# Perceiver block on one core: softplus and the choice of experts spread out in the fourth batch of a tile

## The chip, the core and the metric

One core of one Trainium2 chip runs the whole program. The metric is the device time in microseconds; lower is better. The engines are called as in the profile: PE (TensorE), DVE (VectorE), ACT (ScalarE), POOL (GpSimd), SP (SyncE, which only starts transfers here).

## The reference

The inputs are `x` (128 sequences of 32 tokens of width 256), a context of 257 tokens for each sequence, a mask, and float32 weights. Three layers follow one another, each with a layer norm before it and a residual after it:

```python
x = x + xattn(layernorm(x), ctx, mask)   # 16 heads of 16; softmax over 257 context tokens
x = x + ssd(layernorm(x))                # in this use only batch 0's states are read: out = Y[0] / norm
x = x + moe(layernorm(x))                # 8 experts, top 2, hidden 704, silu gate
```

Two small pieces of it matter here. In the second layer `dt = softplus(dt + dt_bias)`, `A = A_param * dt`, and `cumA = cumsum(A)` over the 32 tokens. In the third the router's 8 logits of each token give the two largest and their numbers, and a one-hot row of 8 for each.

## The kernel before

**Stages.** The first stage (about 1000 us) does the attention, the second layer and the routing of all 4096 tokens. It goes over 32 tiles of 128 tokens; a tile has four batches `b` (one sequence each, all 16 heads). The second stage (about 470 us) runs 71 slots of 128 tokens through the experts. The change is in the first stage alone.

**Order of the work.** Each engine has its instructions in one order written out by hand, and the engines meet at semaphores. Tiles 0 to 3 and 29 to 34 are unrolled on DVE and PE, tiles 4 to 28 are a hardware loop. The work of one tile is spread over several: while tile `i` is in attention, tile `i-1` is in the output projection, second layer norm, `softplus` and cumulative sum, and tile `i-2` in the third norm, the logits and the choice of experts. In batch `b` of tile `i` DVE does the score maxima of the next batch (`maxima`, one operation for each of four groups, L879), copies the keys of the batch after next from PSUM (`take_keys`, two operations, L868), and takes the attention output of this batch (`take_output`: `om`, L892, then `ou`, L894).

**The fourth batch** (`b == 3`). DVE also computes `softplus` of tile `i-1` on vectors of 128x16 in the tile `dtv`. With `u = exp(-|x|)` from ACT it makes `y = u/(u+2)` (`softplus_ratio`, L964 to L966), squares it and starts a polynomial (`softplus_series`, L972 and L973), does six more steps of it (L976, called k1 to k6 below), and closes with L980, L981 and L984. Every one of these reads what the one before wrote and waits for its semaphore. L984 increments `a_done`. In the same batch `take_logits` (L1023) copies the logits of tile `i-2` out of the PSUM bank `M`, and `select` does six operations on 128x8 or smaller (L1028 to L1039).

**PE in the fourth batch**: the scores of the next batch, the keys of the one after (`k`), the router, the weighted values, four transposes of the probabilities, `turn_z1(i+2)` (two transposes into `M`, L493, after `lg_done` of the logits), `project_v` (12 products), four more transposes, and last `sum_a(i-1)`, a product with 128x16 that waits first for `z1T_done` and then for `a_done`. Behind it stands the first batch of the next tile, which begins with its scores.

**ACT in the fourth batch**: exponentials of the four groups, `take_probs`, then `take_rp` (a 32x32 copy that waits for `ou_done`), `take_z1T` (which gives `z1T_done`), `take_values`, `take_probs`, and `decays` after `sum_a`.

**POOL**: in the third batch it does the first norm of tile `i+2` (L1239), in tiles 4 to 27 also `piece_low` (L1289, a 128x512 subtraction that prepares 1/24 of the experts' down weights), then, for the next batches, `split_low` (L1249, 128x516) and `lay_queries` (L1257 and L1261).

Of the kernel before, what the change touches and what calls it, by code (L numbers as in the profile page):

```python
# [8 lines left out]
ALU = mybir.AluOpType  # L9
# [7 lines left out]
NH = D // P  # L17
# [22 lines left out]
ATANH = [2 * k + 1 for k in range(7, 0, -1)]  # L40
# [20 lines left out]
def held(eng, met, *waits):  # L61


    for _, value in waits:
        if not isinstance(value, int):
            eng.compute_val(value)
    eng.wait_ge(*met)
    for sem, value in waits:
        at_least(eng, sem, value)
# [40 lines left out]
def runs(i):  # L110

    return not isinstance(i, int) or 0 <= i < NT


def attend(nc, xd, ctxd, ctxl, maskd, pard, wxbcd, cond, padd, wgd, wud, wdd, d_high, d_low, zbuf, table, outd, con, cst, wg, wu, wd,
# [7 lines left out]
    with own:  # L123
# [71 lines left out]
        dtv = sb("dtv", [P, 11, H])  # L195
# [12 lines left out]
        def carve(n):  # L208
# [47 lines left out]
        dt_ready, dt_done, nabs_done, u_done, soft, a_done = (sem("dt_ready"), sem("dt_done"), sem("nabs_done"),  # L256
                                                              sem("u_done"), sem("soft"), sem("a_done"))
# [12 lines left out]
        init, soft_sum, soft_max = sem("init"), sem("soft_sum"), sem("soft_max")  # L270
        NSOFT = len(ATANH) + 5
# [587 lines left out]
        def _(dve):  # L859
            V = nc.vector  # L860

            def take_keys(i, b):

                n = 4 * i + b
                at_least(dve, s_ready, 4 * n - 4)
                dve.wait_ge(k_ready, n + 1)
                for a in range(NH):
                    V.tensor_scalar(kT[:, b % 2, a, 0:LAST], K2[:, a, :], prm("bk")[:, a:a + 1], None, ALU.add  # L868
                                    ).then_inc(k_done, 1)

            def maxima(i, b, *groups):
                n = 4 * i + b
                for g in groups:
                    if g == 0:

                        held(dve, (init, 2), (msk_in[b], 64 * (i + 1)), (exp_done, 4 * n), (s_ready, 4 * n + 1))
                    else:
                        held(dve, (init, 2), (s_ready, 4 * n + g + 1))
                    V.tensor_tensor_reduce(sm[:, g, :], SC[g][:, 0:S], msk[:, b, :], -1.0, 3.0e38, ALU.add, ALU.min,  # L879
                                           nmx[:, g:g + 1]).then_inc(max_done, 1)  # L880
# [5 lines left out]
                V.reciprocal(rr[:, 0, :], rsum[:, :]).then_inc(rec_done, 1)  # L886

            def take_output(i, b):
                n = 4 * i + b
                dve.wait_ge(o_ready, n + 1)  # L890
                at_least(dve, ou_done, n)
                V.tensor_scalar(om[:, :, :], OT[:, :, 0, :], own2[:, 0:1], None, ALU.mult).then_inc(om_done, 1)  # L892
                dve.wait_ge(om_done, n + 1)
                V.scalar_tensor_tensor(ou[:, :, b * Q:(b + 1) * Q], OT[:, :, 1, :], own2[:, 1:2], om[:, :, :],  # L894
                                       ALU.mult, ALU.add).then_inc(ou_done, 1)
# [58 lines left out]
            su, sr, sy, sw, ss = dtv[:, 2, :], dtv[:, 3, :], dtv[:, 4, :], dtv[:, 8, :], dtv[:, 9, :]  # L954

            def link(ins, j, k):

                ins.then_inc(soft, 1)
                dve.wait_ge(soft, NSOFT * j + k)
# [8 lines left out]
            def softplus_series(j, first, last):  # L968

                if first == 0:  # L970
                    dve.wait_ge(soft, NSOFT * j + 3)
                    link(V.tensor_tensor(sw, sy, sy, ALU.mult), j, 4)  # L972
                    V.tensor_scalar(ss, sw, 1.0 / ATANH[0], None, ALU.mult).then_inc(soft, 1)  # L973
                for k in range(max(first, 1), last):
                    dve.wait_ge(soft, NSOFT * j + 4 + k)
                    V.scalar_tensor_tensor(ss, ss, 1.0 / ATANH[k], sw, ALU.add, ALU.mult).then_inc(soft, 1)  # L976

            def softplus_end(j):
                dve.wait_ge(soft, NSOFT * j + NSOFT - 1)
                link(V.scalar_tensor_tensor(ss, ss, 1.0, sy, ALU.add, ALU.mult), j, NSOFT)  # L980
                V.scalar_tensor_tensor(sw, ss, 2.0, dtv[:, 10, :], ALU.mult, ALU.add).then_inc(soft_sum, 1)  # L981
                dve.wait_ge(soft_sum, j + 1)
                at_least(dve, cum_ready, j)
                V.tensor_tensor(dtv[:, 5, :], sw, prm("apar"), ALU.mult).then_inc(a_done, 1)  # L984
# [36 lines left out]
            def take_logits(j):  # L1021
                dve.wait_ge(lg_ready, j + 1)
                V.tensor_copy(lg[:, 0, :], M[:, 0:E]).then_inc(lg_done, 1)  # L1023

            def select(j):

                held(dve, (init, 2), (lg_done, j + 1))
                V.max(lg[:, 1, :], lg[:, 0, :]).then_inc(top_done, 1)  # L1028
                held(dve, (init, 2), (top_done, j + 1))
                V.max_index(mi[:, :], lg[:, 1, :], lg[:, 0, :]).then_inc(index_done, 1)  # L1030
                V.tensor_tensor(sv[:, 0, 0:1], lg[:, 1, 1:2], lg[:, 1, 0:1], ALU.subtract).then_inc(diff_done, 1)
                dve.wait_ge(index_done, j + 1)
                V.tensor_copy(sv[:, 2, :], mi[:, 0:TOPK]).then_inc(expert_done, 1)
                dve.wait_ge(expert_done, j + 1)
                V.tensor_tensor(oh[:, :, :], cst("iota8").unsqueeze(1).broadcast_to([P, TOPK, E]),
                                sv[:, 2, :].unsqueeze(2).broadcast_to([P, TOPK, E]), ALU.is_equal).then_inc(oh_done, 1)
                dve.wait_ge(oh_done, j + 1)
                at_least(dve, chosen_done, j + 1)
                V.tensor_tensor(lg[:, 2, :], oh[:, 0, :], oh[:, 1, :], ALU.add).then_inc(mm_done, 1)  # L1039
# [103 lines left out]
            def tile(i):  # L1143
                for b in range(TB):
                    nxt, two = following(i, b), following(i, b, 2)
                    if b == 3 and runs(i - 1):
                        softplus_ratio(i - 1)
                        softplus_series(i - 1, 0, 1)
                    if runs(nxt[0]):
                        maxima(*nxt, 0, 1)  # L1150
                    if runs(nxt[0]):
                        maxima(*nxt, 2, 3)
                    if b == 0 and runs(i - 1):
                        weigh(i - 1)
                    if b == 2 and runs(i + 1):
                        take_queries(i + 1)
                    if b == 3 and runs(i - 2):
                        take_logits(i - 2)
                    if runs(two[0]):
                        take_keys(*two)  # L1160
                    if runs(i):
                        take_output(i, b)
                    if b == 3 and runs(i - 1):
                        softplus_series(i - 1, 1, len(ATANH))
                    if b == 0 and runs(i - 1):
                        attention_out(i - 1)
                    if b == 1 and runs(i - 1):
                        normalise2(i - 1)
                    if b == 2 and runs(i - 2):
                        normalise3(i - 2)  # L1170
                    if b == 3 and runs(i - 1):
                        softplus_end(i - 1)
                    if runs(nxt[0]):
                        reciprocals(*nxt)
                    if b == 3 and runs(i - 2):
                        select(i - 2)
                    if b == 0 and runs(i - 2):
                        norms(i - 2)
                    if b == 0 and runs(i - 3):
                        take_ranks(i - 3)  # L1180
                    if b == 0 and isinstance(i, int) and i == 2:
                        ssd()
                    if b == 1 and runs(i - 2):
                        residual2(i - 2)
                    if b == 2 and runs(i - 1):
                        soft_in(i - 1)
                    if b == 0 and runs(i - 2):
                        scale_y(i - 2)
                    if b == 1 and runs(i - 3):
                        place(i - 3)  # L1190
                    if b == 1 and runs(i + 2):
                        statistics1(i + 2)
                    if b == 0 and runs(i - 1):
                        residual1(i - 1)
                        statistics2(i - 1)
# [16 lines left out]
                V.tensor_scalar(kl[:, a, :], M2K[:, a, :], prm("bk")[:, a:a + 1], None, ALU.add).then_inc(vl_done, 1)  # L1212
            take_queries(0)
            statistics1(1)
            take_keys(0, 0)
            maxima(0, 0, 0, 1, 2, 3)
            take_keys(0, 1)
            dve.wait_ge(own_done, 1)
            reciprocals(0, 0)
            steps(dve, tile)  # L1220
# [488 lines left out]
```

## Time and profile before

| | |
|---|---|
| median of 3 runs | 1527.64 us (1525.33 to 1528.3) |
| the profiled execution's own time | 1529.16 us |
| its span | 1527.2 us |
| busy: PE, DVE, ACT, POOL | 93%, 74%, 66%, 55% |
| granted PE clock, mean | 0.969 |

The span is the stretch from the first to the last instruction of the profiled execution; some 2 us of that execution lie outside it. The busy shares are means over both stages.

### The profile page before, as it was taken

What the parts mean: (1) busy time and instruction counts of PE and PEld (TensorE: products, weight loads), DVE (VectorE), ACT (ScalarE), POOL (GpSimd) and SP (SyncE); (2) the same over time, 40 slices, a digit from 0 to 9 for tenths busy, and PEclk for the clock granted to TensorE, in tenths of its full rate; (3) what the DMA queues carried; (4) which work ended last, traced back from release to release, by engine and by line L of the source; (5) the groups of instructions that cost most, each with busy time, mean ns of one, the idle gap of its engine ahead of it and who ended that gap; (6) DMA issues with size and microseconds to landing.
All of it is one profiled execution on the core that took longest, in us unless ns stands there. A gap on an engine that the chain in (4) does not pass through costs nothing.

```text
span 1527.2 us, 53971 instructions
## 1 busy us (share of the span) xinstructions
PE 1422.5 (93%) x15668; PEld 1294.9 (85%) x15669; DVE 1125.5 (74%) x3967; ACT 1000.9 (66%) x2482; POOL 838.1 (55%) x1401
## 2 busy tenths in 40 slices
PE   6969999999999999999999999649999999999997
PEld 5858888888888888888888888449999999999997
DVE  3647777777777777777777777557877787787775
ACT  4726766767766766766766676237777777677674
POOL 4514655655655655565565554226665666566554
PEclk9969999999999999999999999569999999999999
DMA  5302544554333343343343331425555555556554
GB/s 187 81 12 81 167 140 130 165 159 128 110 103 90 98 114 90 88 119 88 97 117 86 87 81 41 180 78 160 143 162 140 155 145 160 138 144 161 137 141 111
DMA packets 102009, 183.81 MB, mean 120 GB/s; under 512 B 19392, under 2 KB 61376, under 8 KB 101792
## 3 DMA queue, kind: packets, MB, share of 16 engines
q1 hardware_dynamic: 86272, 164.35, 35.2%
q0 software_dynamic: 15680, 18.76, 7.0%
q8 instruction: 29, 0.48, 0.1%
q14 instruction: 28, 0.23, 0.0%
HBM read 152.63 MB, written 31.13 MB: 120 GB/s over the span
## 4 chain that ended last, share of the span: by engine, by line
PE 72%; DVE 8%; issue 6%; ACT 2%; DMA 2%; POOL 1%; POOLq 1%; DVEq 0%; ACTq 0%; SPq 0%
PE m L412 12%; PE k L412 10%; PE y_p L1420 9%; PE v_p L412 9%; PE up_p L1420 8%; PE gate_p L1420 8%; PE sc L412 7%; PE pt L471 5%; PE ht_p L1459 3%; DVE dtv L976 2%; DMA par<-zbuf,gi 2%; ACT wd L735 1%; PE m L493 1%; PE z_p L1426 1%; DVE kT L868 1%
## 5 line engine op out<-in xcount | busy, mean ns | idle before, releaser
L735 ACT ACTIVATE wd<-wd,nmx 128x257 f32<-128x257 f32 x512 | 254.7, 499 | 100.6 <-DVE nmx L879 97.2
L879 DVE CUSTOM_DVE_ANT_0 wd<-sc,wd 128x257 f32<-128x257 f32 x512 | 187.3, 422 | 56.1 <-PE sc L412 45.8
L1622 POOL DMA_INDIRECT out<-par,oi x71 | 113.5, 1599 | 146.7 <-ACT par L1528 146.1
L1249 POOL TENSOR_TENSOR ctx_lo<-wd,ctx_hi 128x516 fp32r<-128x516 f32 x128 | 165.3, 1291 | 48.9 <-ACT ctx_hi L711 44.1
L711 ACT ACTIVATE wd<-pt 128x512 f32<-128x512 f32 x256 | 151.5, 592 | 57.9 <-PE pt L471 57.7
L471 PE MATMUL pt<-con,wd 128*128 128x128 f32 x1024 | 161.0, 280 | 3.0 <-ACT wd L735 0.7
L412 PE MATMUL k<-ctx_hi,wkh 128*128 128x256 f32 x512 | 158.2, 309 | 1.4 <-POOL ctx_lo L1249 1.4
L412 PE MATMUL v_p<-wvh,ctx_hi 128*128 128x256 f32 x512 | 158.0, 309 | 0.5 <-ACT y L711 0.5
L1499 ACT ACTIVATE uw_hi<-wu 128x1408 fp32r x71 | 98.3, 1385 | 85.1 <-PE up_p L1420 84.8
L1610 POOL COPY oi<-par 128x4 int32 x71 | 148.2, 2088 | 0.0
L1557 DVE TENSOR_TENSOR uw_lo<-wu,uw_hi 128x1408 fp32r<-128x1408 f32 x71 | 115.4, 1626 | 41.2 <-ACT uw_hi L1499 41.2
L412 PE MATMUL k<-ctx_lo,wkh 128*128 128x256 f32 x512 | 144.7, 283 | 0.0
L412 PE MATMUL v_p<-wvh,ctx_lo 128*128 128x256 f32 x512 | 144.6, 282 | 0.0
L412 PE MATMUL k<-ctx_hi,wkl 128*128 128x256 f32 x512 | 144.4, 282 | 0.0
L1557 DVE TENSOR_TENSOR gw_lo<-wg,gw_hi 128x1408 fp32r<-128x1408 f32 x71 | 115.4, 1625 | 39.3 <-ACT gw_hi L1499 39.3
L412 PE MATMUL v_p<-wvl,ctx_hi 128*128 128x256 f32 x512 | 143.9, 281 | 0.0
L412 PEld LDWEIGHTS k<-ctx_hi,wkh 128*128 128x128 f32 x512 | 96.4, 188 | 50.5 <-issue 48.7
L1610 POOL COPY gi<-par 128x4 int32 x71 | 122.3, 1722 | 9.5 <-issue 5.7
L1267 POOL TENSOR_TENSOR rr<-wd,rr 128x4 f32<-128x4 f32 x128 | 25.6, 200 | 178.9 <-DVE rr L886 178.9
L1420 PE MATMUL y_p<-wd,hT_hi 128*128 x426 | 121.0, 284 | 1.9 <-DVE hT_lo L1557 1.9
L471 PEld LDWEIGHTS pt<-con,wd 128*128 128x128 f32 x1024 | 113.0, 140 | 10.1 <-ACT wd L735 5.9
L1420 PE MATMUL y_p<-wd,hT_lo 128*128 x426 | 120.4, 283 | 0.0
(197 smaller groups left out, 4662.2 us busy)
## 6 DMA issues: line engine op xcount, KB each, us to landing
dl<-d_low SPq DMA_DIRECT2D x71, 768.0 KB, 4.4
wd<-in_ctx SPq DMA_DIRECT2D x128, 258.0 KB, 2.8
wd<-in_mask SPq DMA_DIRECT2D x512, 32.1 KB, 1.8
wd<-in_wd SPq DMA_DIRECT2D x24, 256.0 KB, 3.0
d_high<-wd SPq DMA_DIRECT2D x24, 256.0 KB, 2.0
d_low<-wd SPq DMA_DIRECT2D x24, 256.0 KB, 2.3
wd<-d_high SPq DMA_DIRECT2D x8, 768.0 KB, 9.1
wg<-in_wg SPq DMA_DIRECT2D x8, 704.0 KB
```

The costliest lines, as they stand in the source:

```text
L412: return nc.tensor.matmul(out, lhsT, rhs, start=start, stop=stop)
L471: last = nc.tensor.transpose(PT[:, o:o + P], pr[:, g, t * P:(t + 1) * P], ident)
L711: return nc.scalar.activation(out, in_, ACT.Copy, **kw)
L735: nc.scalar.activation(pr[:, g, :], sm[:, g, :], ACT.Exp, bias=nmx[:, g:g + 1], scale=-1.0, accum_out=rsum[:, g:g + 1]).then_inc(exp_done, 1)
L879: V.tensor_tensor_reduce(sm[:, g, :], SC[g][:, 0:S], msk[:, b, :], -1.0, 3.0e38, ALU.add, ALU.min, nmx[:, g:g + 1]).then_inc(max_done, 1)
L1249: G.tensor_tensor(ctx_lo[:, b % 2], ctx[:, b], ctx_hi[:, b % 2].bitcast(F32), ALU.subtract).then_inc(lo_done, 1)
L1420: return nc.tensor.matmul(out, lhsT, rhs, start=start, stop=stop)
L1459: last = nc.tensor.transpose(HB[k][:, (c % 4) * P:(c % 4 + 1) * P], hb[:, c * P:(c + 1) * P], ident)
L1499: nc.scalar.activation(dst, src, ACT.Copy).then_inc(done, 1)
L1557: V.tensor_tensor(dst, src, hi.bitcast(F32), ALU.subtract).then_inc(done, 1)
L1610: G.tensor_copy(dst.unsqueeze(1), tab[:, bass.ds(col, 1), :]).then_inc(done, 1)
L1622: G.indirect_dma_start(outd[:, :], bass.IndirectOffsetOnAxis(oi[:, s, 1:2].bitcast(U32), 0), yb[:, s, :], None, compute_op=ALU.add).then_i ...
```

## The change

The steps of `softplus` and of `select` are no longer done as blocks. `take_keys` and `take_output` are cut into their single operations, `softplus_end` and `select` into functions of one or two operations, and in the fourth batch they alternate. All operations, their operands and their semaphores stay; only their order on DVE changes, in the fourth batch alone. The other engines' programs are the same.

```diff
-            def take_keys(i, b):
+            def take_keys(i, b, *chunks):
...
-                for a in range(NH):
+                for a in chunks:
...
             def take_output(i, b):
+                first_head(i, b)
+                second_head(i, b)
...
+            def softplus_log(j):
+                dve.wait_ge(soft, NSOFT * j + NSOFT - 1)
+                V.scalar_tensor_tensor(ss, ss, 1.0, sy, ALU.add, ALU.mult).then_inc(soft, 1)
+
+            def softplus_sum(j):
+                dve.wait_ge(soft, NSOFT * j + NSOFT)
+                V.scalar_tensor_tensor(sw, ss, 2.0, dtv[:, 10, :], ALU.mult, ALU.add).then_inc(soft_sum, 1)
...
             def softplus_end(j):
...
                 dve.wait_ge(soft_sum, j + 1)
                 at_least(dve, cum_ready, j)
                 V.tensor_tensor(dtv[:, 5, :], sw, prm("apar"), ALU.mult).then_inc(a_done, 1)
```

The order on DVE in the fourth batch of a tile in the loop, one operation or group of operations after another (`k1` is `softplus_series(i-1, 1, 2)`, and so on; `top` is `V.max`; `index` is `V.max_index` and the subtraction behind it; `number` is the cast of the two numbers; `log`, `sum`, `end` are L980, L981, L984):

```
before: ratio square | max0 max1 max2 max3 | logits | keys0 keys1 | om ou | k1 k2 k3 k4 k5 k6 | log sum end |
        reciprocals | top index number one_hot both
after:  ratio square | max0 max1 k1 max2 k2 max3 k3 | logits k4 | keys0 k5 top | keys1 k6 index | om log ou |
        sum number end one_hot | reciprocals | both
```

## Rows read from the trace of the kernel before

**Rows 1.** Waits of PE over the whole span: total us, times, longest.

```profile
PE m L412 <- DVE dtv L984: 16.4, 28, 2.5
PE sc L412 <- issue: 14.8, 27, 0.8
```

**Rows 2.** Windows: tiles 5 to 27 of the loop, then one unrolled tile; each engine's busy us.

```profile
188.70:856.80 668.10, 641.07 (x8632) 559.91 (x8631) 520.08 (x2502) 462.02 (x1423) 389.96 (x803) 1.00 0.39 114
...
886.00:914.00 28.00, 27.87 (x384) 24.41 (x390) 21.75 (x108) 19.22 (x60) 15.53 (x35) 1.00 0.29 73
```

**Rows 3.** Timeline of PE in tile 19, fourth batch: start us, us, line, tiles, count, idle before.

```profile
620.98 0.38 PE L493 MATMUL m<-con,wd 128*128 128x128 f32 x2
...
622.62 0.60 PE L471 MATMUL pt<-con,wd 128*128 128x128 f32 x4
623.68 0.37 PE L412 MATMUL m<-dtv,con 128*128 128x16 f32 x2 [0.47 <-DVE dtv L984]
624.59 0.69 PE L412 MATMUL sc<-kT,qbd 32*64 32x257 f32 x16 [0.54 <-issue]
```

**Rows 4.** Timeline of DVE in the same batch.

```profile
618.80 0.42 DVE L879 CUSTOM_DVE_ANT_0 wd<-sc,wd 128x257 f32<-128x257 f32 x1
...
619.15 0.42 DVE L879 CUSTOM_DVE_ANT_0 wd<-sc,wd 128x257 f32<-128x257 f32 x1
...
619.97 0.17 DVE L1023 COPY lg<-m 128x8 f32<-128x8 f32 x1 [0.39 <-PE m L412]
620.16 0.88 DVE L868 TENSOR_SCALAR kT<-k,par 128x256 f32<-128x256 f32 x2
620.96 0.28 DVE L892 TENSOR_SCALAR om<-sc,own 128x64 f32<-128x64 f32 x1
621.27 0.28 DVE L894 SCALAR_TENSOR_TENSOR ou<-sc,own,om 128x64 f32<-128x64 f32 x1
621.47 1.44 DVE L976 SCALAR_TENSOR_TENSOR dtv<-dtv 128x16 f32<-128x16 f32 x6
...
623.36 0.18 DVE L984 TENSOR_TENSOR dtv<-dtv,par 128x16 f32<-128x16 f32 x1
623.46 0.18 DVE L886 RECIPROCAL rr<-rsum 128x4 f32<-128x4 f32 x1
```

**Rows 5.** Timeline of ACT in the same batch.

```profile
621.67 0.17 ACT L711 ACTIVATE rp<-sc 32x32 f32<-32x32 f32 x1
621.75 0.36 ACT L711 ACTIVATE wd<-m 128x256 f32<-128x256 f32 x1
```

**Rows 6.** Timeline of POOL in the same batch and just before it.

```profile
617.75 1.23 POOL L1239 TENSOR_SCALAR wd<-wd,mv,rs 128x256 f32<-128x256 f32 x1 [0.17 <-issue]
618.95 1.28 POOL L1289 TENSOR_TENSOR wd<-wd 128x512 fp32r<-128x512 f32 x1
620.19 1.28 POOL L1249 TENSOR_TENSOR ctx_lo<-wd,ctx_hi 128x516 fp32r<-128x516 f32 x1
621.43 0.40 POOL L1257 TENSOR_TENSOR qbd<-wd,own 128x128 f32<-128x128 f32 x1
621.77 0.19 POOL L1261 COPY kT<-wd 128x4 f32 x1
```

**Rows 7.** First series step alone (lines view, last columns busy us, mean ns); DVE and POOL, tile 28.

```profile
L976 DVE SCALAR_TENSOR_TENSOR dtv<-dtv 128x16 f32<-128x16 f32 x1 | 0.4, 393 | 0.0
...
883.32 1.21 DVE L976 SCALAR_TENSOR_TENSOR dtv<-dtv 128x16 f32<-128x16 f32 x6
...
882.04 0.41 POOL L1257 TENSOR_TENSOR qbd<-wd,own 128x128 f32<-128x128 f32 x1
```

**Rows 8.** Timelines of DVE and POOL, first batch of a tile; POOL elsewhere.

```profile
514.47 0.43 DVE L996 TENSOR_TENSOR yn<-y,dtv 128x256 f32<-128x256 f32 x1
...
514.35 0.62 POOL L1271 TENSOR_TENSOR px<-rr,con 128x16 f32<-128x16 f32 x2
...
616.41 0.39 POOL L1271 TENSOR_TENSOR px<-rr,con 128x16 f32<-128x16 f32 x2
```

More of the change, by code:

```diff
@@ L888, in take_output, with first_head @@
             def take_output(i, b):
+                first_head(i, b)
+                second_head(i, b)
+            def first_head(i, b):
                 n = 4 * i + b
@@ L892, in take_output, with second_head @@
                 V.tensor_scalar(om[:, :, :], OT[:, :, 0, :], own2[:, 0:1], None, ALU.mult).then_inc(om_done, 1)
+            def second_head(i, b):
+                n = 4 * i + b
                 dve.wait_ge(om_done, n + 1)
@@ L976, in softplus_series @@
                     V.scalar_tensor_tensor(ss, ss, 1.0 / ATANH[k], sw, ALU.add, ALU.mult).then_inc(soft, 1)
+            def softplus_log(j):
[4 more added lines that the diff above has]
+                V.scalar_tensor_tensor(sw, ss, 2.0, dtv[:, 10, :], ALU.mult, ALU.add).then_inc(soft_sum, 1)
             def softplus_end(j):
-                dve.wait_ge(soft, NSOFT * j + NSOFT - 1)
-                link(V.scalar_tensor_tensor(ss, ss, 1.0, sy, ALU.add, ALU.mult), j, NSOFT)
-                V.scalar_tensor_tensor(sw, ss, 2.0, dtv[:, 10, :], ALU.mult, ALU.add).then_inc(soft_sum, 1)
                 dve.wait_ge(soft_sum, j + 1)
@@ L1023, in take_logits, with select_top, select_index @@
                 V.tensor_copy(lg[:, 0, :], M[:, 0:E]).then_inc(lg_done, 1)
-            def select(j):
+            def select_top(j):
                 held(dve, (init, 2), (lg_done, j + 1))
                 V.max(lg[:, 1, :], lg[:, 0, :]).then_inc(top_done, 1)
+            def select_index(j):
                 held(dve, (init, 2), (top_done, j + 1))
@@ L1031, in select, with select_number, select_one_hot @@
                 V.tensor_tensor(sv[:, 0, 0:1], lg[:, 1, 1:2], lg[:, 1, 0:1], ALU.subtract).then_inc(diff_done, 1)
+            def select_number(j):
                 dve.wait_ge(index_done, j + 1)
                 V.tensor_copy(sv[:, 2, :], mi[:, 0:TOPK]).then_inc(expert_done, 1)
+            def select_one_hot(j):
                 dve.wait_ge(expert_done, j + 1)
@@ L1036, in select, with select_both @@
                                 sv[:, 2, :].unsqueeze(2).broadcast_to([P, TOPK, E]), ALU.is_equal).then_inc(oh_done, 1)
+            def select_both(j):
                 dve.wait_ge(oh_done, j + 1)
@@ L1145, in tile @@
                     nxt, two = following(i, b), following(i, b, 2)
-                    if b == 3 and runs(i - 1):
+                    soft_now = b == 3 and runs(i - 1)
+                    pick_now = b == 3 and runs(i - 2)
+                    if soft_now:
                         softplus_ratio(i - 1)
@@ L1150, in tile @@
                         maxima(*nxt, 0, 1)
+                    if soft_now:
+                        softplus_series(i - 1, 1, 2)
                     if runs(nxt[0]):
-                        maxima(*nxt, 2, 3)
+                        maxima(*nxt, 2)
+                    if soft_now:
+                        softplus_series(i - 1, 2, 3)
+                    if runs(nxt[0]):
+                        maxima(*nxt, 3)
+                    if soft_now:
+                        softplus_series(i - 1, 3, 4)
                     if b == 0 and runs(i - 1):
@@ L1156, in tile @@
                         take_queries(i + 1)
-                    if b == 3 and runs(i - 2):
+                    if pick_now:
                         take_logits(i - 2)
+                    if soft_now:
+                        softplus_series(i - 1, 4, 5)
                     if runs(two[0]):
-                        take_keys(*two)
-                    if runs(i):
-                        take_output(i, b)
-                    if b == 3 and runs(i - 1):
-                        softplus_series(i - 1, 1, len(ATANH))
+                        take_keys(*two, 0)
+                    if soft_now:
+                        softplus_series(i - 1, 5, 6)
+                    if pick_now:
+                        select_top(i - 2)
+                    if runs(two[0]):
+                        take_keys(*two, 1)
+                    if soft_now:
+                        softplus_series(i - 1, 6, len(ATANH))
+                    if pick_now:
+                        select_index(i - 2)
+                    if runs(i):
+                        first_head(i, b)
+                    if soft_now:
+                        softplus_log(i - 1)
+                    if runs(i):
+                        second_head(i, b)
+                    if soft_now:
+                        softplus_sum(i - 1)
+                    if pick_now:
+                        select_number(i - 2)
+                    if soft_now:
+                        softplus_end(i - 1)
+                    if pick_now:
+                        select_one_hot(i - 2)
                     if b == 0 and runs(i - 1):
@@ L1170, in tile @@
                         normalise3(i - 2)
-                    if b == 3 and runs(i - 1):
-                        softplus_end(i - 1)
                     if runs(nxt[0]):
                         reciprocals(*nxt)
-                    if b == 3 and runs(i - 2):
-                        select(i - 2)
+                    if pick_now:
+                        select_both(i - 2)
                     if b == 0 and runs(i - 2):
@@ L1214, in _ @@
             statistics1(1)
-            take_keys(0, 0)
+            take_keys(0, 0, 0, 1)
             maxima(0, 0, 0, 1, 2, 3)
-            take_keys(0, 1)
+            take_keys(0, 1, 0, 1)
             dve.wait_ge(own_done, 1)
```

## Prediction, made before the changed kernel ran

> **What bounds the kernel now.** I read the waits of PE first, because PE is the busy engine in nearly every slice. Two lines stand out: PE waited 16.4 us in 28 places for L984, the last step of `softplus`, and 14.8 us in 27 places before the scores with nothing shown that it waited for [rows 1]. Both belong to one place, the border between two tiles. The windows say what the border costs: 23 tiles of the loop took 668.1 us, 29.05 us each, an unrolled tile 28.0 us, with nearly the same PE work in each (641.07/23 = 27.87 us and 27.87 us) [rows 2]. So this stage goes at PE's pace and loses about 1 us a tile, at the border.
>
> The timeline shows how. In tile 19 PE's last transposes end at 623.22, `sum_a` starts at 623.68, and the scores of the next tile only at 624.59 [rows 3]. L984 ended at 623.54 [rows 4], so `sum_a` follows 0.14 behind it and the scores 1.05. I take the 1.05 us as a fixed delay behind the last semaphore that `sum_a` waits for: in the loop PE's sequencer must come round to the next tile there. PE itself is free at 623.22 and needs 0.37 for `sum_a` [rows 3], so at best the scores start at 623.59, 1.0 us sooner. The release is what DVE's order sets: before L984 DVE does logits, two keys, `om`, `ou`, six series steps and L980, L981, one behind the other from 619.97 on [rows 4].
>
> **The change, step by step, if nothing else interfered.** Nothing is added: the same operations, semaphores and transfers, in another order on DVE's queue alone. A small step that waits for the one before it costs 0.21 us from start to start (six steps in 1.21 us, less the last one's 0.175, over five) [rows 7]. A small operation behind an unrelated one costs 0.10 (623.36 to 623.46) [rows 4]; I take 0.12, and 0.15 for the two behind the logits, where the keys came 0.19 after [rows 4]. Now place them in tile 19. k1 to k3 go between the maxima and cost 0.36 us, which the 0.39 us of waiting for the router swallows [rows 4]: logits stay at 619.97. Then k4 620.12, keys0 620.27, k5 620.67 (a key copy costs 0.40 [rows 4]), top 620.79, keys1 620.91, k6 621.31, index (0.28 for its three short operations, an estimate from the 0.10) to 621.71, `om` 621.71, log inside the 0.31 us between `om` and `ou` [rows 4], `ou` 622.02, sum 622.22, number 622.32, end 622.43 to 622.60. `a_done` is 0.94 us earlier. But `ou` is 0.75 us later, and ACT copies `rp` 0.40 behind `ou`'s start and then does the `z1T` copy, 0.08 later and 0.36 long [rows 5]: it ends at 622.86. PE waits for that too before `sum_a`, so this is what is late next, and the release moves from 623.54 to 622.86: 0.68 us, taken as 0.65 gained a tile.
>
> **What else is running there.** This is the step on which the forecast turns. Each series step reads two operands from SBUF (`ss` and `sw`). POOL works without a break from 617.75 to 621.96, on four operations that also read SBUF [rows 6]. The present order puts the series almost wholly behind them; the new order puts k1 to k4 right among them. The trace has such a meeting. k1 started at 621.47 while POOL's L1257 (621.43 to 621.83) ran, and took 393 ns where the others take 175; it ended 0.09 us after POOL's next operation started (621.77) [rows 6, 7]. In tile 28, where L1257 started at 882.04, over before the series began at 883.32, six steps took 1.21 us instead of 1.44 [rows 4, 7]. I find the held step in each of the 24 tiles that have L1289 and in none of the others. The reverse is there too: POOL's pair of L1271 took 0.62 us where DVE's L996, which reads two SBUF operands, ran over it, and 0.39 elsewhere [rows 8]. Operations with one operand in PSUM, the keys and `ou`, pass L1249 and L1257 at 0.88 and 0.28 us [rows 4, 6], unharmed. So I read: a DVE operation with two SBUF inputs that comes while a POOL operation reads SBUF stands until that one is through, and DVE's queue stands behind it. The longest hold that the trace shows is 0.22 us (393 less 175); for L1289 and L1249, 1.24 us from start to start, no row shows one. The bounds are 0 (POOL's long operations let DVE in) and the rest of the POOL operation; I take the second, for L1257 held k1 to its end.
>
> The page "SBUF — State Buffer" of the Trainium skill, section "Who interferes with whom", says this as a rule: a DVE instruction with two SBUF inputs contends with a GpSimd instruction that reads SBUF, and the one that comes second blocks fully until the first is done. By that rule the change loses, and the trace agrees as far as L1257 and L1271 go; for the long operations no row can say.
>
> **The sum with the hold**, in tile 19 and the other 23 tiles with L1289. k1 stands where the third maximum started, at 618.80 [rows 4], and waits out the end of L1239, to about 619.03. max2 618.96. k2 at 619.31 (a maximum takes 0.35, 618.80 to 619.15 [rows 4]) falls into L1289 and ends 0.09 behind the start of L1249, at 620.28. max3 620.23. k3 at 620.58 falls into L1249 and ends, POOL having slipped 0.03, at 621.55. Logits 621.48 instead of 619.97: `turn_z1`, at 620.98 [rows 3], must wait for them until about 621.8, so a new stall of 0.8 us stands before `project_v`. k4 at 621.60 is held by L1257 to 621.89. From there on POOL is done: keys0 621.82, k5 622.22, top, keys1 622.44, k6 622.84, index, `om` 623.24, `ou` 623.55, sum, number, end 623.96 to 624.14. `ou` is 2.28 us late, `rp` follows at 623.95 and the `z1T` copy at 624.03 to 624.39. The release is at 624.39 instead of 623.54: 0.85 us lost. DVE's own next maxima, ACT's exponentials and POOL's next work follow PE's scores and slide with them; the third group's exponential is not touched and the fourth starts 0.6 later, which the transposes at 622.62 still leave room for.
>
> 24 x 0.85 = 20.4 us. In tiles 2, 3, 28 and 29 L1289 is missing and only k2 meets L1249: about 0.15 us each, 0.6. The last two tiles with a `softplus` have no maxima and no keys; PE's longest waits for L984, up to 2.5 us, are there [rows 1], and steps of the series now run while DVE waits for the router and the heads. I take back 1.9 us of 0 to 5. Together +19.1 us: 1529.16 becomes 1548.3 for the profiled execution; the median of the runs is 1.5 lower, so **1547 us**. The expert stage starts later and is otherwise the same.
>
> **The rivals.**
> 1. *The hold, but not into the gaps.* If k1 misses the gap before L1289, the row of holds shifts: k1 to 620.3, k2 to 621.5, k3 to 621.9, a release about 1.2 us late, 24 x 1.2 = 29: 1555. If DVE gets in only when POOL is idle, k1 stands until 621.86 and everything behind it moves, maxima 2 and 3 too: about 1.9 a tile, 1572. Against it: k1 got in between L1257 and L1261 in 24 tiles, and L1261 was not later for it.
> 2. *No hold by the long operations* (the other side): then 24 x 0.65 = 15.6, about 3 in the other tiles and 1.9 at the end, 20.5 us faster: 1507. For it: no row shows L1289 or L1249 holding anything. Against it: they are the same operation as L1257, only longer. It decides where the holds of one tile sum to less than 0.9 us (0.65 gained and 0.25 of slack before the logits); I expect 2.1.
> 3. *Short holds*, at most 0.22 us each as in rows 7: the early ones vanish in that slack, the release is 0.1 us sooner than now, with the border tiles about 6 us faster: 1521.
> 4. *Nothing gained by interleaving*: each placed step costs its full 0.21 us. Then the logits come 0.24 late, the release 0.15 late, 3.6 us, less the end's 1.9: 1529, no change. The row against it is the 0.10 from L984 to L886 [rows 4]. The Trainium skill states this one ("VectorE: DVE Perf Modes", "The DRAIN you can't avoid"): the next operation does not start until the pipeline is empty, and a semaphore between costs nothing extra; the trace does not agree, with 0.10 against 0.21.
>
> **How the numbers follow.** The hold into the gaps has 0.50 (1541 to 1555 by itself, for 0.6 to 1.2 us a tile), missed gaps 0.13, starved 0.10, no hold 0.15, short holds 0.07, no gain from interleaving 0.03, and 0.02 is left. The range from 1520 to 1574 holds all but the case without a hold and what is left. A measurement here tells about 0.2%, 3 us: faster 0.22 (no hold and short holds), within it 0.05, slower 0.73.
>
> **What would show it.** In the loop three of the six L976 steps at 0.9 to 1.0 us (k2, k3) and 0.3 (k4), each ending just behind a start of POOL; L1023 at 1.5 us later than now; PE waiting some 0.8 us for it before L493, 24 times; a wait for the `z1T` copy before `sum_a`; a period near 29.9 us. If k2 and k3 take 175 ns, the hold is wrong and rival 2 holds; if the holds are there but PE doesn't wait for the logits, the sizes are wrong. What would make it wrong besides: POOL reaching these operations at another time, or the 1.05 us behind the release not being fixed.

## The result, and the profile after

The change made the kernel slower, by 0.5%: 1536.26 us (median of 5 runs, 1534.97 to 1538.52) against 1527.64 (5 runs), a ratio of 1.0053, interval 1.0039 to 1.0067. The forecast was 1547. The holds of k2, k3 and k4 are where it put them, of the size that it gave them; what they cost a tile is little more than half of what it said.

The waits of PE in the changed kernel (total us, times, longest):

```profile
PE m L493 <- DVE lg L1035: 13.6, 24, 0.6
PE sc L412 <- issue: 13.2, 26, 0.8
PE m L412 <- DVE dtv L996: 4.0, 3, 2.0
PE m L412 <- ACT wd L711: 3.7, 20, 0.5
```

The wait for the last step of `softplus` (16.4 us in 28 places [rows 1]) has all but gone. In its place stand a wait for the logits, 24 times, and one for the `z1T` copy (`ACT wd L711`). Lines are renumbered: L983 is k1 to k6, L1035 the logits, L896 and L901 `om` and `ou`, L996 the end; on POOL L1289 is the norm, L1339 `piece_low`, L1299 `split_low`, L1307 the 128x128 product.

The same tile's fourth batch on DVE. It lies 7.16 us later than in [rows 4] (its first maximum starts at 625.27, there at 618.11):

```profile
625.97 0.17 DVE L983 SCALAR_TENSOR_TENSOR dtv<-dtv 128x16 f32<-128x16 f32 x1
...
626.40 1.02 DVE L983 SCALAR_TENSOR_TENSOR dtv<-dtv 128x16 f32<-128x16 f32 x1
627.35 0.41 DVE L879 CUSTOM_DVE_ANT_0 wd<-sc,wd 128x257 f32<-128x257 f32 x1
...
627.69 0.97 DVE L983 SCALAR_TENSOR_TENSOR dtv<-dtv 128x16 f32<-128x16 f32 x1
628.59 0.15 DVE L1035 COPY lg<-m 128x8 f32<-128x8 f32 x1
628.70 0.32 DVE L983 SCALAR_TENSOR_TENSOR dtv<-dtv 128x16 f32<-128x16 f32 x1
628.95 0.47 DVE L868 TENSOR_SCALAR kT<-k,par 128x256 f32<-128x256 f32 x1
...
630.17 0.27 DVE L896 TENSOR_SCALAR om<-sc,own 128x64 f32<-128x64 f32 x1
...
630.48 0.28 DVE L901 SCALAR_TENSOR_TENSOR ou<-sc,own,om 128x64 f32<-128x64 f32 x1
...
630.88 0.18 DVE L996 TENSOR_TENSOR dtv<-dtv,par 128x16 f32<-128x16 f32 x1
```

and on POOL:

```profile
624.91 1.23 POOL L1289 TENSOR_SCALAR wd<-wd,mv,rs 128x256 f32<-128x256 f32 x1 [0.17 <-issue]
626.12 1.28 POOL L1339 TENSOR_TENSOR wd<-wd 128x512 fp32r<-128x512 f32 x1
627.35 1.28 POOL L1299 TENSOR_TENSOR ctx_lo<-wd,ctx_hi 128x516 fp32r<-128x516 f32 x1
628.59 0.39 POOL L1307 TENSOR_TENSOR qbd<-wd,own 128x128 f32<-128x128 f32 x1
628.94 0.18 POOL L1311 COPY kT<-wd 128x4 f32 x1
```

Read the two together. k2 starts inside L1339 and ends at 627.42, 0.07 behind the start of L1299; k3 starts inside L1299 and ends at 628.66, 0.07 behind the start of L1307; k4 starts inside L1307 and ends at 629.02, 0.08 behind the start of L1311. A step of 0.17 us stands until the POOL operation that it met is through. k1 started 0.17 before the norm was over and lost nothing. The `rp` and `z1T` copies on ACT, and then PE:

```profile
630.80 0.19 ACT L711 ACTIVATE rp<-sc 32x32 f32<-32x32 f32 x1 [1.86 <-DVE ou L901]
630.89 0.38 ACT L711 ACTIVATE wd<-m 128x256 f32<-128x256 f32 x1
```

```profile
628.87 0.43 PE L493 MATMUL m<-con,wd 128*128 128x128 f32 x2 [0.57 <-DVE lg L1035]
630.57 0.60 PE L471 MATMUL pt<-con,wd 128*128 128x128 f32 x4
631.32 0.40 PE L412 MATMUL m<-dtv,con 128*128 128x16 f32 x2
632.25 0.69 PE L412 MATMUL sc<-kT,qbd 32*64 32x257 f32 x16 [0.53 <-issue]
```

Counted from the batch's first maximum, the scores start 6.98 us later; before it was 6.48 (624.59 less 618.11). That is 0.50 in this tile. The mean of the loop is a little less. The window from the first maximum of tile 5 to that of tile 28 has

```profile
189.72:869.60 679.88, 647.57 (x8649) 559.95 (x8649) 530.13 (x2508) 459.78 (x1426) 390.87 (x806) 1.00 0.38 112
```

29.56 us a tile, where the same window of the kernel before has 669.63 us, 29.11 (the window of [rows 2] is 1.5 us short of it). So 0.45 is lost a tile, 10.2 us in these 23, and 10.6 with tile 4. The rest of the 7.1 us between the spans (1534.3 and 1527.2) comes out so: the fourth batch of tile 0, which the change does not touch, begins 1.5 us later (44.94 against 43.45; over all the kernels of this document it begins between 42.7 and 46.7, so this is scatter of the start), tiles 1 to 3 win 0.8, tiles 28 and 29 win 0.4, the last two tiles 1.9, and the expert stage is 1.9 shorter.

### The profile page after: what moved, and what is told of

It is laid out like the page before. It is cut to its first block, busy times and chain, and to the rows that moved or that the text cites. A ratio compares the mean times of both kernels' runs of the same rounds, so it can differ in the third digit from the quotient of the medians.

```text
span 1534.3 us, 54097 instructions
## 1 busy us (share of the span) xinstructions
PE 1428.0 (93%) x15668; PEld 1293.6 (84%) x15669; DVE 1134.6 (74%) x3967; ACT 997.7 (65%) x2482; POOL 837.8 (55%) x1401
## 4 chain that ended last, share of the span: by engine, by line
PE 69%; issue 8%; DVE 8%; ACT 3%; DMA 2%; POOL 1%; DVEq 1%; POOLq 1%; ACTq 0%; SPq 0%
PE m L412 11%; PE y_p L1470 9%; PE v_p L412 9%; PE up_p L1470 8%; PE gate_p L1470 8%; PE k L412 7%; PE sc L412 7%; PE pt L471 5%; PE ht_p L1509 2%; DVE dtv L983 2%; DMA par<-zbuf,gi 2%; ACT wd L735 1%; PE m L493 1%; PE z_p L1476 1%; DVE wd L879 1%
## 5 line engine op out<-in xcount | busy, mean ns | idle before, releaser
L879 DVE CUSTOM_DVE_ANT_0 wd<-sc,wd 128x257 f32<-128x257 f32 x512 | 191.6, 422 | 79.8 <-PE sc L412 72.6
L1299 POOL TENSOR_TENSOR ctx_lo<-wd,ctx_hi 128x516 fp32r<-128x516 f32 x128 | 165.0, 1289 | 49.8 <-ACT ctx_hi L711 46.3
L711 ACT ACTIVATE wd<-pt 128x512 f32<-128x512 f32 x256 | 151.7, 592 | 49.6 <-PE pt L471 49.5
```

What stands on the lines that cost most here:

```text
L711: return nc.scalar.activation(out, in_, ACT.Copy, **kw)
L1299: G.tensor_tensor(ctx_lo[:, b % 2], ctx[:, b], ctx_hi[:, b % 2].bitcast(F32), ALU.subtract).then_inc(lo_done, 1)
```

## Experiments

Each ratio is against the kernel before on the same chip; a period is that of the loop, from maximum to maximum as above. Periods of different experiments can come from different chips (1 and 4 from one, 2 and 3 from a second, 5 and `after_logits` from a third, `logits_filled` and 7 from a fourth), and the only trace of the unchanged kernel is that of the result; so where a period and a ratio disagree, the ratio counts. In all, L983 (L976 in the old order) has 192 instances.

**1. One input from SBUF instead of two** (`after_one_input`, and `before_one_input` in the old order).

```diff
-    V.scalar_tensor_tensor(ss, ss, 1.0 / ATANH[k], sw, ALU.add, ALU.mult)
+    V.tensor_scalar(ss, ss, 1.0 / ATANH[k], 0.05, ALU.add, ALU.mult)
```

> The changed kernel, with the six series steps k1 to k6 as operations with one SBUF input: (ss + c) * 0.05 in place of (ss + c) * sw. The value of softplus is so only approximated; order, semaphores, sizes are the same. Theory (a DVE operation with two SBUF inputs stands while POOL reads SBUF): all L983 take about 175 ns, none over 200; the logits wait for PE again; PE has no wait for them; the release of sum_a comes about 1 us sooner than in the kernel before, so 20 to 25 us faster than before: 1503 to 1508 us. Rival (the new order itself costs, since each placed step takes its time from the big operations): nothing changes against the changed kernel, 1536 us.

> The kernel before, with the same replacement in its six series steps (softplus only approximated). Theory: only k1 was held there, 0.22 us in 24 tiles, and it stands on the chain to sum_a: 5 us faster, 1522 to 1523 us, L976 at most 180 ns. Rival (the 393 ns of k1 have another cause than its second SBUF input): k1 stays at 393 ns and the time at 1527 to 1528 us.

Measured: 1.0047 (1.0033 to 1.0060) and 1.0001 (0.9992 to 1.0011). The steps are held as before, in the changed order

```profile
629.67 1.05 DVE L983 TENSOR_SCALAR dtv<-dtv 128x16 f32<-128x16 f32 x1
630.64 0.41 DVE L879 CUSTOM_DVE_ANT_0 wd<-sc,wd 128x257 f32<-128x257 f32 x1
630.98 0.98 DVE L983 TENSOR_SCALAR dtv<-dtv 128x16 f32<-128x16 f32 x1
```

Here k1 is 0.41 us in the loop of the old order, k2 1.05 and k3 0.98 in the changed one. So "two inputs from SBUF" is not the whole condition: a `tensor_scalar` with one is held as well. Both expectations missed.

**2. Steps as reductions** (`after_reduce_steps`), again one input, another operation; POOL at full size.

```diff
-    V.scalar_tensor_tensor(ss, ss, 1.0 / ATANH[k], sw, ALU.add, ALU.mult)
+    V.tensor_reduce(ss, ss.unsqueeze(2), AX.X, ALU.add)
```

> The changed kernel with k1 to k6 as tensor_reduce over an axis of one (one SBUF input; the polynomial of softplus is left out, its first term stays). The steps with one SBUF input of the run before were tensor_scalar and were held 1.05, 0.98 and 0.32 us. If any ordinary DVE operation from SBUF to SBUF is held while POOL's subtraction runs, these are too, and the time is that of the changed kernel. If tensor_scalar is a special case, they take about 150 ns each and the time is some 20 us under before.

One run alone, of 1507.18 us (the kernel before has 1534.86 on this chip), period 28.48. DVE, and then the POOL operation that runs beside the first two:

```profile
607.80 0.16 DVE L983 TENSOR_REDUCE dtv<-dtv 128x16 f32<-128x16 f32 x1
...
608.22 0.16 DVE L983 TENSOR_REDUCE dtv<-dtv 128x16 f32<-128x16 f32 x1
...
610.01 0.41 DVE L1045 TENSOR_TENSOR sv<-lg 128x1 f32<-128x1 f32 x1
```

```profile
607.53 1.28 POOL L1339 TENSOR_TENSOR wd<-wd 128x512 fp32r<-128x512 f32 x1
```

Two reductions pass inside L1339 in 0.16 us each. In the same kernel the 128x1 subtraction of the selection, two inputs from SBUF, stands 0.41 instead of 0.14. Without the holds the places of the steps cost nothing; the meeting of their form of operation with POOL's is what costs.

**3. POOL's long subtractions cut to a sixteenth** (`after_short_pool`, `before_short_pool`), and **turned into writes only** (`after_pool_memset`).

```diff
-    G.tensor_tensor(ctx_lo[:, b % 2], ctx[:, b], ctx_hi[:, b % 2].bitcast(F32), ALU.subtract)
+    G.tensor_tensor(ctx_lo[:, b % 2, :, 0:16], ctx[:, b, :, 0:16], ..., ALU.subtract)    # short
+    G.memset(ctx_lo[:, b % 2].bitcast(F32), 0.0)                                         # memset
```

(`piece_low` likewise. Both short kernels also clear the three target tiles once, at the start.)

> The changed kernel with POOL's two long subtractions cut to a sixteenth of their columns (L1339 128x32, L1299 128x32; the low halves of the context and of the experts' down weights are so left out but for those columns, and are zero). DVE's program is that of the changed kernel. Theory (POOL's long two-input operations hold DVE's steps): L983 at 160 to 180 ns, no wait of PE for the logits, scores at best 1 us sooner a tile than in the kernel before; 20 to 25 us faster than before, ratio 0.984 to 0.987. Rival (the new order itself delays the logits and ou, POOL only happens to run then): ratio stays at 1.005.

> The kernel before with the same cut in POOL's two subtractions. Theory: L976 is never held (k1 0.22 us sooner), 24 x 0.22 = 5 us: ratio 0.996 to 0.997. With the run of the changed order beside it the difference of the two is what the new order gives when nothing holds it: theory 16 to 20 us. Rival: ratio 1.000, and the two orders 8 us apart the other way.

> The changed kernel with POOL's two long subtractions replaced by memsets of the same outputs (full size; the low halves are zero, so products with them add nothing). A memset reads nothing. Theory A (a hold comes from POOL reading SBUF): L983 at 160 to 180 ns, ratio 0.984 to 0.987, although POOL writes 128x516. Theory B (any long POOL operation that touches SBUF holds DVE): k2 and k3 are held as long as the memsets last, ratio above 0.99.

Measured: 0.9799 (0.9785 to 0.9812), 0.9951 (0.9937 to 0.9964) and 0.9791 (0.9776 to 0.9806). With short POOL operations the new order is 1.5% faster than the old one (0.9799/0.9951), some 24 us; with them as they are it is 0.5% slower. All three gained a little more than expected (0.984 to 0.987, and 0.996 to 0.997 for the old order). The writing operations do not hold; k3 starts inside one of them:

```profile
605.69 0.52 POOL L1299 MEMSET ctx_lo<- 128x516 f32 x1
```

```profile
605.97 0.17 DVE L983 SCALAR_TENSOR_TENSOR dtv<-dtv 128x16 f32<-128x16 f32 x1
```

And the 1.05 us behind the release are not fixed. With the release early, PE's loop work lies under its last transposes (short kernel):

```profile
605.46 0.60 PE L471 MATMUL pt<-con,wd 128*128 128x128 f32 x4
605.89 0.29 PE L412 MATMUL m<-dtv,con 128*128 128x16 f32 x2
606.39 0.69 PE L412 MATMUL sc<-kT,qbd 32*64 32x257 f32 x16 [0.20 <-issue]
```

The `z1T` copy, the later of the two that `sum_a` waits for, ended at 605.45, so the scores follow 0.94 behind it. But the idle PE saw before them is 0.20, not 0.54.

**4. The selection alone placed, the series in its block** (`select_only`), and **the `z1T` copy ahead of `rp` on ACT** (`z1T_before_rp`).

```diff
-    softplus_series(i - 1, 1, 2) ... softplus_series(i - 1, 6, len(ATANH)), softplus_log(i - 1)   # in their places
+    softplus_series(i - 1, 1, len(ATANH)); softplus_log(i - 1)                                     # behind second_head
```

> The changed kernel, but k1 to k6 and log stand in one block behind ou, as before; only the steps of the choice of experts are placed (top, index, number, one_hot). Theory: no step of the series is held any more, ou comes 0.35 us later than before, k1 is past L1257 (0.22 us back), so the release is about 0.1 us later than before: 1528 to 1531 us. Rival (the operations of the choice in front of ou are what costs): most of the loss stays, 1534 to 1537 us.

> The changed kernel, with one exchange on ACT in the fourth batch: the z1T copy before the rp copy, so that it no longer waits for ou. Theory: the z1T copy, ending at 631.27 in tile 19, is what releases sum_a; without it a_done at 631.06 does, and the scores come about 0.14 us sooner: 3 us faster than the changed kernel, about 1533 us. Rival (a_done is the release anyway): no change, 1536 us.

Measured: 1.0068 (1.0054 to 1.0082) and 1.0047 (1.0034 to 1.0061). The first misses both of its expectations, the second lies between its two and settles neither. In `select_only` no series step is held (L983 at most 178 ns), but L1045 stands 0.35 instead of 0.13 inside `split_low`, `a_done` comes 5.67 us behind the first maximum where it was 5.43, and PE's wait for it grew:

```profile
PE m L412 <- DVE dtv L996: 25.1, 31, 3.3
```

Placed before `ou` the selection only delays the chain that PE waits for. That is 0.24 us a tile, 5.8 in 24, and three tiles lost another 1.4 each (see 6): together about the 10 us of the ratio. In `z1T_before_rp` the scores came 0.08 sooner behind the first maximum. That is all there was to win: in the changed kernel PE's last transposes end at 631.17 and `sum_a` starts at 631.32, so without the `z1T` copy it could start some 0.1 sooner. 24 times 0.08 is 2 us, 0.13%, and this the two ratios (1.0047 and 1.0053, each to about 0.0014) can't tell.

In both kernels the batch behind the border takes 8.60 us between first maxima, against 8.40 in the two kernels of the result. The runs point to the chip, not to the order: the old order has 8.54 on the same chip (`before_one_input`) and 8.59 on that of experiment 3 (`before_short_pool`, which is all the same 0.5% faster than the kernel before there), and the three orders on the chip of experiment 5 have 8.40. No kernel was profiled on two chips, so this is argued and not shown, and what makes the difference stays open.

**5. `piece_low` moved on POOL** ahead of the last operations of the third batch (`before_moved`, `after_moved`).

```diff
+                    if b == 2 and k is not None:
+                        piece_low(k)
                     ... last_probs of the third batch ...
-                    if b == 2 and k is not None:
-                        piece_low(k)
```

> The kernel before with the same move of piece_low and nothing else. The first series step (k1) no longer meets POOL's 128x128 product, since POOL is done earlier: L976 goes from a mean of 202 ns to about 175, 0.22 us a tile sooner, 24 tiles, -5 us: ratio 0.996 to 0.997. Rival, that the hold of k1 costs nothing in the end: ratio 1.000.

> The changed kernel, with POOL's piece_low (the 128x512 subtraction) moved ahead of last_probs in the third batch; nothing is left out. If the long subtractions of POOL are what holds the placed steps, and the place of the step against them sets the price: only one step (k2 or k3) meets a long subtraction (split_low), about 1.1 us held instead of 1.6 in two pieces, the logits are hardly late, PE waits for them little, the release of sum_a is some 0.2 us earlier than in the kernel before: ratio about 0.995 against the kernel before on the same chip. Rival, that the interleaving itself is what costs (its place in DVE's queue, not what POOL does at that time): ratio stays at 1.005.

Measured: 0.9966 (0.9954 to 0.9978) and 1.0001 (0.9992 to 1.0010). In the old order k1 is 165 ns instead of 393 in the loop and the period 0.25 shorter, all as expected: the little hold of [rows 7] had cost 5 us. In the new order k2 alone meets a long operation and is held longer than I thought, 1.19; PE still waits 0.28 for the logits in 24 places (6.7 us), and the ratio, 0.5% above the expected one, misses. k1 lies wholly inside POOL's norm in this kernel, and is not held:

```profile
620.81 0.17 DVE L983 SCALAR_TENSOR_TENSOR dtv<-dtv 128x16 f32<-128x16 f32 x1
...
621.24 1.19 DVE L983 SCALAR_TENSOR_TENSOR dtv<-dtv 128x16 f32<-128x16 f32 x1
```

```profile
619.91 1.23 POOL L1289 TENSOR_SCALAR wd<-wd,mv,rs 128x256 f32<-128x256 f32 x1 [0.17 <-issue]
621.11 1.29 POOL L1299 TENSOR_TENSOR ctx_lo<-wd,ctx_hi 128x516 fp32r<-128x516 f32 x1
```

**6. k2 and k3 behind the logits** (`after_logits`), and the same **with PE's wait filled** (`logits_filled`).

```diff
-    softplus_series(i - 1, 2, 3) behind the third maximum, (3, 4) behind the fourth, (4, 5) behind the logits
+    softplus_series(i - 1, 2, 5) behind the logits
```

```diff
                     if runs(i + 2):
+                        pe.wait_ge(k_done, 8 * i + 12)        # logits_filled only
+                        for f in range(3):
+                            mm(K2[:, 0, :], cst("trib"), wo[:, 0, :])
                         pe.wait_ge(z1T_done, i + 3)
```

> The changed kernel, but k2 and k3 stand behind the logits, with k4, instead of between the maxima and before the logits. Nothing is left out. The logits are then on time, and PE's wait for them (13.6 us in 24 places) must be gone. If the time is set by the release of sum_a alone: k2 is held by split_low, k3 by the 128x128 product, everything behind them ends at the same time as in the changed kernel or 0.2 us later, PE's wait only moves to sum_a (for the z1T copy or L996): ratio 1.005 to 1.009. Rival, that the stall before L493 is itself the loss: 13.6 us come back, ratio about 0.996.

> The kernel after_logits, with three more products (128x128 by 128x256, into the bank of the keys, their result is never read) that PE does while it waits for the z1T copy before sum_a. Nothing is left out, and no release is earlier or later. Theory: in after_logits PE stood still for 0.95 us before sum_a and for 0.53 behind it, and its granted clock was then at half for some 3.5 us in 18 of 24 tiles; with the wait filled the clock stays at 1.00 and all tiles take 29.56 us, as in the changed kernel: ratio 1.005 to 1.007 against the kernel before, where after_logits had 1.022. Rival, that something else slows these tiles (the series' place itself, a transfer): ratio stays at 1.022.

`after_logits` is 1.0220 (1.0199 to 1.0242), far off both expectations. The wait for the logits is gone, as it had to be. The wait moved to `sum_a`, and the scores start 6.99 us behind the first maximum, as in the changed kernel (6.98):

```profile
648.43 0.40 PE L412 MATMUL m<-dtv,con 128*128 128x16 f32 x2 [0.95 <-ACT wd L711]
649.36 0.69 PE L412 MATMUL sc<-kT,qbd 32*64 32x257 f32 x16 [0.53 <-issue]
```

Yet most of its tiles take 31.1 us. The windows of the next microseconds show why (the third figure from the end is PE's granted clock):

```profile
650.00:651.00 1.00, 1.00 (x14) 1.00 (x8) 0.82 (x5) 0.21 (x2) 0.69 (x2) 0.78 0.68 197
651.00:652.00 1.00, 1.00 (x6) 1.00 (x6) 0.65 (x4) 1.00 (x5) 0.98 (x2) 0.50 0.22 72
```

After the border, where PE stood 0.95 us and then 0.53, the granted clock was 0.50, the lower level of 1.2 GHz, until about 654. About one tile in four kept the full clock, and took 29.56 us: the changed kernel's period. With three idle products in the wait (`logits_filled`) PE looks like this:

```profile
634.86 1.46 PE L412 MATMUL k<-par,con 128*128 128x256 f32 x6
636.15 0.29 PE L412 MATMUL m<-dtv,con 128*128 128x16 f32 x2
636.85 0.69 PE L412 MATMUL sc<-kT,qbd 32*64 32x257 f32 x16 [0.41 <-issue]
```

The granted clock is 1.00 in the whole loop, all tiles of the loop take 29.7, and the ratio is 1.0086 (1.0073 to 1.0099). It gives back 1.3 of 1.7% by doing more work. That it stays above the expected 1.005 to 1.007 is the unrolled tiles: tiles 2, 3, 28 and 29 take 28.84 to 28.91 here and 27.63 to 28.12 in `after_logits`, 4.0 us together, 0.26% (why the added products cost so much there is not traced). In the loop 0.10 of the 0.13 us a tile above the changed kernel lies in the batch behind the border, 8.50 on this chip.

**7. Fewer steps placed** (`few`), and with `piece_low` moved (`few_moved`). On DVE: k1 behind the second maximum, k2 between the keys, k3 behind them, k4 between `om` and `ou`, the rest of the series as a block behind `ou`, the selection behind all.

```diff
-    max2 k2 max3 k3 | logits k4 | keys0 k5 top | keys1 k6 index | om log ou | sum number end one_hot | ...
+    max2 max3 | logits | keys0 k2 keys1 k3 | om k4 ou | k5 k6 log sum end | top index number one_hot ...
```

> The order of few_moved on DVE (k1 behind the second maximum, k2 between the keys, k3 behind them, k4 between om and ou, the rest of the series as a block behind ou, the selection behind all), with POOL's piece_low where it was in the kernel before. Nothing is left out. By the theory, k1 runs in the gap before piece_low (174 ns, as in the changed kernel), k2 between the keys now meets split_low (1.28 us, it ends about 3.3 us behind the first maximum) and is held from 2.3 to 3.3, k3 meets the 128x128 product a little (0.2); the logits are on time; ou about 1.3 us later than before, a_done and the z1T copy about 0.3 to 0.6 later than in few_moved by 0.8 to 1.0: ratio 0.995 to 1.003, that is most of few_moved's gain needs the moved subtraction. If the order alone made the gain: 0.985.

> piece_low moved as in the two kernels beside it, and on DVE only those steps placed that find an idle spot or a cheap one: k1 behind the second maximum, k2 between the two keys, k3 behind the second key, k4 between om and ou; k5, k6, log, sum, end behind ou as a block, all of the selection behind them as before. Nothing is left out. By the theory (steps with both operands in SBUF are held by POOL's long subtractions; what counts is the later of a_done and the z1T copy behind ou): k1 and k2 may be held a little, logits on time, ou 0.4 us later than before, a_done about 0.6 to 0.8 us earlier, scores sooner by as much: -14 to -21 us, ratio 0.986 to 0.991, faster than both kernels. If the interleaving itself costs: 1.000 or more.

`few_moved` is **0.9850** (0.9837 to 0.9864), 1505.52 us against 1528.88: faster than both kernels, and by a little more than the expected 0.986 to 0.991. No step in the loop is over 0.23 us, the logits are on time, and PE does not wait for the release:

```profile
610.20 0.60 PE L471 MATMUL pt<-con,wd 128*128 128x128 f32 x4
610.63 0.29 PE L412 MATMUL m<-dtv,con 128*128 128x16 f32 x2
611.34 0.69 PE L412 MATMUL sc<-kT,qbd 32*64 32x257 f32 x16 [0.42 <-issue]
```

`few` is 1.0033 (1.0021 to 1.0045), just above the upper edge of the expected. k2 starts between the keys inside `split_low` and stands 0.93; the scores still start 0.07 sooner behind the first maximum than before, but the batch behind the border takes 8.96, where `logits_filled` has 8.50 on the same chip. In it PE pauses 0.33 (start to start) in the middle of the 32 weighted-value products with no wait shown; its cause stays open. 24 times 0.46 is 11 us, 0.7%, so this pause, and not the hold alone, keeps the order alone from a gain. As measured, the order alone gains nothing, the moved subtraction alone 0.34%, both 1.5%.

## Why the prediction was right in direction and wrong in size

- **The hold by the long operations, into the gaps**: right in the mechanism, in the place and in the size. k2 1.02, k3 0.97 and k4 0.32 us, against 0.9 to 1.0 and 0.3; k3 and k4 so in 24 tiles; logits at 621.43 in the time of [rows 4], predicted 621.48. Rival 1's missed gap is excluded by the 0.07 us behind each POOL start, its starved case too; rivals 2 and 3 by the durations. One small part was wrong: k1 was to stand until the norm was over, and ran in 0.17 inside it; that cost nothing in the sum.
- **The term "0.85 us lost" a tile is the step that failed.** It measured 0.50 in tile 19 and 0.45 in the mean of the loop, so the 24 tiles lost 10.6 us instead of 20.4. It was mis-sized in three places, here in tile 19. The small operations behind unrelated ones cost 0.08 each (629.34, 629.42, 629.50 start one behind the other), not 0.10 to 0.12, and the three of `index` 0.20 (629.97 to 630.17), not 0.28, so `ou` started 5.21 us behind the first maximum and not 5.44: 0.23. `rp` came 0.32 behind `ou`, not 0.40 (the copy ended 0.03 later behind it): 0.05. And the scores came 0.98 behind the end of the copy, not 1.05: 0.07. Together 0.35, from 0.85 to 0.50. A row for the first stood in [rows 4]: 623.36 to 623.46 is 0.10, and I rounded it up.
- **PE's wait for the logits**: right, 24 times, 0.57 against 0.8; it moves PE's `project_v` but, as the sum had it, not the time (experiment 6: without this wait the tiles at full clock have the same period).
- **What is late next**: `ou`, `rp`, the `z1T` copy. Right; it ends 0.21 behind L996 (631.27 against 631.06). But PE's own transposes, moved back by its wait for the logits, end at 631.17, so they come next at once; putting the copy first (experiment 4) brought 0.08 of these 0.21.
- **"No hold" gives 20.5 us of gain**: tested at 24 (experiment 3), so the order itself is worth what its purpose says. The 0.65 per tile was low (the periods of the two short kernels, on one chip, differ by 0.81), because the delay behind the release is partly PE's own idle time, which an early release hides.
- **The other tiles, +0.6**: wrong in sign. Tiles 2, 3, 28 and 29 won 0.30, 0.30, 0.12 and 0.25, though k2 is held there as the sum had it (0.94 to 1.04 us); all that lies outside the 24 tiles and ahead of the last two comes to +0.3 only by luck, through the 1.5 of scatter at the start. **The last two, -1.9**: measured -1.9, a guess between 0 and 5 that happened to fit. **"The expert stage is otherwise the same"**: it was 1.9 us shorter, without a test of why. PE's waits for gathered rows were 17.0 us against 18.3. The granted clock is a rival, and the likelier for most of it: in this stage it was at 0.50 for 3.4 us twice in the kernel before (from 1300.0 and from 1419.5) and once in the changed one (from 1308.8); work of 1.7 us that takes 3.4 there makes 1.7 of the 1.9, an estimate.
- **Rival 4**, nothing gained by interleaving: false, by 0.08 to 0.11 a step. The section of the Trainium skill that the prediction names for it also says that a next operation which is not held starts earlier, so it is no witness for this rival.
- **The stated cause** was too narrow and too wide. The Trainium skill, "SBUF — State Buffer", "Who interferes with whom", says that `tensor_scalar` may contend too, in its two-port modes, that `tensor_reduce` never does on this chip, and that a GpSimd instruction that only writes does not meet DVE's second input. The runs agree with all three (1.05, 0.16 and 0.17 us). Its rule would also have POOL's norm, which reads SBUF, hold k1; in `after_moved` k1 took 0.17 inside it in every tile of the loop, and there the measurement decides.

## What to carry to other kernels

Before placing a small VectorE operation in a gap, lay GpSimd's timeline beside it: the price of the gap is not the operation's own 0.1 to 0.2 us but the rest of the GpSimd operation that it meets, when that is a `tensor_tensor` from SBUF and the VectorE operation reads two SBUF operands (or is a `tensor_scalar`). Then move the GpSimd operation, not only the VectorE one: here each alone gave +0.3% and -0.3%, both together -1.5%. And where a wait of PE can't be removed, look what the granted clock does behind it: 0.95 and 0.53 us idle at one border brought it to 0.50 in three tiles of four, 0.57 idle 2 us ahead of the border and 0.15 and 0.53 at it never did. Whether the place of the idle time or its sum (1.48 against 1.25) made the difference, these runs do not separate.

## What the runs showed of the hardware that was not expected

- **PE's clock falls behind a border whose scores start no later than in the changed kernel.** From the end of the transposes to the scores there are 1.9 us in `after_logits` (647.48 to 649.36) with 0.40 of work in them; the changed kernel has 1.1 us there, 0.40 of them work, and 0.57 idle some 2 us ahead. The first had the granted clock at 0.50 for about 3.5 us in three of four tiles, 1.5 us lost each time, the second never. `select_only`, with 0.70 and 0.59 idle around `sum_a`, had it in three of its tiles.
- **The hold ends within 0.07 to 0.10 us behind the start of POOL's next operation**, though POOL's operations follow each other without a gap; POOL's own operations are not longer for it (1.28 us with and without). The longest hold is that of k1 in tile 1 of the changed kernel, 1.28 us, the whole of one L1299.
- **A `tensor_tensor` of POOL holds, its `tensor_scalar` did not.** And a hold works on large operations too: with `piece_low` moved, DVE's 128x256 normalisation beside it (`tensor_scalar`) took 0.88 us instead of 0.40; nothing waited for it there.
